# Flamingo cross-attention and experts on one core: another order of a batch, a second bank pair for the first query stack, and ranks in two matmuls

## The reference

```
x = x + tanh(g_xattn) * attention(layernorm(x), ctx, ctx)
x = x + tanh(g_ffn)   * experts(layernorm(x))

attention: q, k, v = projections with biases; softmax(q k' / sqrt(16)) v; output projection with bias
experts:   bids = sigmoid(x conf_w' + conf_b) * wealth
           the two highest bids choose two experts; weights = softmax of these two bids
           sum over the chosen experts of weight * down(silu(gate x) * up x)
```

## Time and profile before

| what | value |
|---|---|
| median of three runs | 1084.73 us (1083.6 to 1086.69) |
| the profiled execution | 1083.07 us, of which 1081.4 us is the span from first to last instruction |
| busy share of the span | PE 93%, DVE 56%, ACT 46%, POOL 34% |
| attention loop, batches 2 to 13 | 98.27 to 398.00 us of the span |
| mean granted clock of PE, share of full speed | 0.969; 1.00 in the loop |

### The profile page before, as it was taken

How to read it: one execution, slowest core, us unless ns; L and a number is a source line. 1 busy time by engine, 2 the same in 40 slices (tenths; PEclk the granted TensorE clock), 3 DMA queues, 4 the chain that set the end, 5 groups by cost and what they waited for, 6 DMA issues and landing times.

```text
span 1081.4 us, 25127 instructions
## 1 busy us (share of the span) xinstructions
PE 1001.3 (93%) x8750; PEld 855.2 (79%) x8750; DVE 610.8 (56%) x1519; ACT 502.0 (46%) x796; POOL 366.3 (34%) x439
## 2 busy tenths in 40 slices
PE   5789999999999997759999999999999999999993
PEld 4556777777777765448999999999799999999993
DVE  3556777777777776455544444444554444444452
ACT  4366777777777774334323232332433323233321
POOL 1124555555555552443322212121332212122121
PEclk8799999999999999869999999999999999999997
DMA  8000111111111119258712111121262212121211
GB/s 254 27 22 22 43 45 47 41 41 41 43 51 58 41 39 371 77 182 323 256 25 40 25 35 35 25 37 23 42 229 49 37 23 40 20 40 23 37 35 17
DMA packets 48338, 77.30 MB, mean 71 GB/s; under 512 B 8616, under 2 KB 42152, under 8 KB 44456
## 3 DMA queue, kind: packets, MB, share of 16 engines
q0 software_dynamic: 18080, 50.15, 16.7%
q1 hardware_dynamic: 30216, 26.62, 8.3%
HBM read 52.09 MB, written 24.40 MB: 71 GB/s over the span
## 4 chain that ended last, share of the span: by engine, by line
PE 81%; ACT 5%; issue 4%; DVE 3%; POOL 3%; DMA 1%; SPq 1%; POOLq 1%; ACTq 0%; DVEq 0%
PE gate L1485 17%; PE up L1485 17%; PE down L1499 11%; PE down L1501 6%; PE pv L590 4%; PE scores L579 4%; PE misc L486 4%; PE scores L540 3%; PE maxps L554 2%; PE misc L513 2%; PE misc L522 2%; POOL K_rest L1204 2%; ACT probs L771 1%; PE misc L624 1%; PE turned L1468 1%
## 5 line engine op out<-in xcount | busy, mean ns | idle before, releaser
L1937 POOL DMA_INDIRECT out<-y,token x64 | 100.9, 1577 | 424.8 <-DVE y L1806 323.8
L1696 ACT ACTIVATE silu<-gate 128x512 f32<-128x512 f32 x128 | 76.8, 600 | 281.6 <-PE up L1485 281.6
L984 DVE TENSOR_REDUCE max_neg<-maxps 128x4 f32<-128x1024 f32 x128 | 156.5, 1222 | 60.2 <-PE maxps L554 60.2
L1485 PE MATMUL gate<-x_hi,w_split 128*128 128x256 f32 x1024 | 185.0, 282 | 2.0 <-DVE x_lo L1772 1.6
L1797 DVE TENSOR_TENSOR h<-silu,up 128x512 f32<-128x512 f32 x128 | 88.1, 688 | 174.8 <-ACT silu L1696 174.8
L1499 PE MATMUL down<-w_split,h_hi 128*128 128x512 f32 x512 | 185.9, 398 | 0.0
L1485 PE MATMUL up<-x_hi,w_split 128*128 128x256 f32 x1024 | 184.4, 282 | 0.0
L771 ACT ACTIVATE probs<-scores 128x1024 f32<-128x1024 f32 x124 | 127.2, 1026 | 80.5 <-PE scores L579 79.5
L1485 PEld LDWEIGHTS gate<-x_hi,w_split 128*128 128x128 f32 x1024 | 149.4, 189 | 5.5 <-issue 2.7
L1485 PEld LDWEIGHTS up<-x_hi,w_split 128*128 128x128 f32 x1024 | 148.8, 189 | 0.0
L1501 PE MATMUL down<-w_split,h_lo 128*128 128x256 f32 x512 | 144.1, 281 | 0.0
(11 more groups left out here) (204 smaller groups left out, 1586.3 us busy)
## 6 DMA issues: line engine op xcount, KB each, us to landing
stage<-gate_up_T POOLq DMA_DIRECT2D x20, 1024.0 KB, 8.1
stage<-down_T POOLq DMA_DIRECT2D x10, 1024.0 KB, 11.1
xg<-dispatched SPq DMA_DIRECT2D x34, 272.0 KB
ctxT<-ctxT SPq DMA_DIRECT2D x17, 256.0 KB, 2.8
x_all<-x SPq DMA_DIRECT2D x16, 256.0 KB, 5.2
out<-x_all SPq DMA_DIRECT2D x16, 256.0 KB, 2.2
dispatched<-pads SPq DMA_DIRECT2D x4, 272.0 KB, 3.6
dispatched<-pads POOLq DMA_DIRECT2D x4, 272.0 KB, 4.3
```

The source lines that it names most:

```text
L984: V.tensor_reduce(to, maxps[:], AX.X, ALU.max, negate=True).then_inc(s["max_taken"], 1)
L1485: last = mm(bank[:, i, :], into_inner(w, pair, mat)[:, c, cols], r[:, c, :], start=m == 0, stop=m == len(terms) - 1)
L1696: nc.scalar.activation(silu[pair % 2][:], gate[pair % 2][:], ACT.Silu).then_inc(s_silu, 1)
L1937: pool.indirect_dma_start(out, bass.IndirectOffsetOnAxis(token[:, t:t + 1], axis=0), y[:, t, :], None, compute_op=ALU.add).then_inc(s_adde ...
```

## The change

Five things change. On TensorE the second half of a turn has another order: W1 now stands ahead of K0, Q's projection ahead of S5, each S5 to S7 ahead of its M5 to M7, W2 ahead of S7, and `logits` ahead of K1. The stack Q0 is written to the bank pair `maxps` (the new view `beside`), and so waits for no unit to be read; Q1 then waits for the read of K1, one unit less. The ranks of both halves of a batch are two matmuls with 16 columns, for which VectorE makes a second slice of `macc`: counts before the batch, and these plus the first half's. ScalarE follows the new order, and VectorE's `positions` now stand ahead of maximum 5. The new view, `stack` and `ranks`:

```
+        beside = maxps[:].rearrange("p u t s -> p (u t) s")
-            def stack(b, what, c, n):
+            def stack(b, what, c, n, to=None):
-                write_unit(n)
+                if to is None:
+                    to = scores
+                    write_unit(n)
-                for t in range(QT):
-                    mm(use.bank("RK")[:, t, 0:EXPERTS], before[:], m12[:, t, :], start=True, stop=False)
-                    if t == 1:
-                        mm(use.bank("RK")[:, t, 0:EXPERTS], ones[:], m12[:, 0, :], start=False, stop=False)
-                    last = mm(use.bank("RK")[:, t, 0:EXPERTS], ones[:], macc[:], start=False, stop=True)
-                last.then_inc(s["misc_written"], 1)
+                mm(use.bank("RK")[:, :, 0:EXPERTS], before[:], m12[:], start=True, stop=False)
+                mm(use.bank("RK")[:, :, 0:EXPERTS], ones[:], macc[:], start=False, stop=True).then_inc(s["misc_written"], 1)
```

In TensorE's `body`:

```
-                    if ahead:
-                        stack(b + 2, what[0], int(what[1]), unit(b, what))
+                    if ahead and what == BESIDE:
+                        stack(b + 2, what[0], int(what[1]), None, beside)
+                    elif ahead:
+                        stack(b + 2, what[0], int(what[1]), unit(b, what) - (1 if UNITS[UNITS.index(what) - 1] == BESIDE else 0))
...
+                weigh(b, par, 1)
                 stack_ahead("K0")
-                weigh(b, par, 1)
-                max_of_next(5)
-                score(b, par, 5)
                 if ahead:
                     project_q(use)
-                score(b, par, 6)
+                score(b, par, 5)
+                max_of_next(5)
                 if back:
                     turn_x2(b - 1, 1 - par, use)
+                score(b, par, 6)
                 max_of_next(6)
+                weigh(b, par, 2)
                 score(b, par, 7)
-                weigh(b, par, 2)
                 max_of_next(7)
-                stack_ahead("K1")
                 if back:
                     logits(use)
+                stack_ahead("K1")
                 if nxt:
                     turn_maxima(b + 1, use)
```

In ScalarE's `body`:

```
+                read_pv(b, 1)
                 stack_ahead("K0")
-                exps(b, 5)
                 if back:
                     norm_x2(b - 1, 1 - par)
-                read_pv(b, 1)
-                exps(b, 6)
+                exps(b, 5)
                 if ahead:
                     read_q(b + 2, use)
-                exps(b, 7)
+                exps(b, 6)
                 if back:
                     read_whole(x2T[:], "TX2", use)
+                exps(b, 7)
                 read_pv(b, 2)
-                stack_ahead("K1")
                 if back:
                     sigmoid(use)
+                stack_ahead("K1")
                 stack_ahead("Q0")
```

On VectorE, the end of `second_choice`, a part of `positions`, and `body`:

```
-                V.tensor_tensor(m12[:], m1[:], m2[:], ALU.add).then_inc(s["masks_ready"], 1)
+                V.tensor_tensor(m12[:], m1[:], m2[:], ALU.add).then_inc(s["masks_made"], 1)
+                dve.wait_ge(s["masks_made"], b + 1)
+                if not is_first(b):
+                    dve.wait_ge(s["rows_ready"], b)
+                V.tensor_tensor(macc[:, 1, :], macc[:, 0, :].bitcast(fp32), m12[:, 0, :].bitcast(fp32), ALU.add).then_inc(s["masks_ready"], 1)
...
-                link(V.tensor_tensor(macc[:], macc[:].bitcast(fp32), m12[:, 0, :].bitcast(fp32), ALU.add))
+                link(V.tensor_tensor(macc[:, 0, :], macc[:, 1, :].bitcast(fp32), m12[:, 1, :].bitcast(fp32), ALU.add))
                 link(V.tensor_tensor(w2[:], w1[:], ed[:], ALU.mult))
-                link(V.tensor_tensor(macc[:], macc[:].bitcast(fp32), m12[:, 1, :].bitcast(fp32), ALU.add))
...
                 max_of_next(4)
-                max_of_next(5)
                 if late:
                     positions(b - 2, par, use)
+                max_of_next(5)
```

More of the change, by code:

```diff
@@ L213, in attention_stage @@
         m12 = sb("m12", [P, QT, EXPERTS], f32r)
-        macc = sb("macc", [P, EXPERTS], f32r)
+        macc = sb("macc", [P, QT, EXPERTS], f32r)
         v1 = sb("v1", [P, QT])
@@ L287, in attention_stage @@
         STACKS = ["K0", "Q0", "K1", "Q1"]
+        BESIDE = "Q0"
         def units_before(b):
@@ L539, in stack @@
                             r = slice(half * STACK, (half + 1) * STACK)
-                            last = mm(scores[:, half * QT + i, :], picks[f"{what} {part}"][r, i, :], source[what][r, c, :],
+                            last = mm(to[:, half * QT + i, :], picks[f"{what} {part}"][r, i, :], source[what][r, c, :],
                                       start=part == "high", stop=part == "rest")
@@ L641, in known_counts @@
                 use.free(pe, "KNOWN")
-                mm(use.bank("KNOWN")[:, 0, 0:EXPERTS], ones[:], macc[:], start=True, stop=True).then_inc(s["misc_written"], 1)
+                mm(use.bank("KNOWN")[:, 0, 0:EXPERTS], ones[:], macc[:, 0, :], start=True, stop=True).then_inc(s["misc_written"], 1)
             pe.wait_ge(s["first_loaded"], 16 * NFIRST)
@@ L752, in count_rows @@
                 EPILOGUE2.free(pe, "COUNT")
-                mm(EPILOGUE2.bank("COUNT")[:, 0, 0:EXPERTS], ones[:], macc[:], start=True, stop=True).then_inc(s["misc_written"], 1)
+                mm(EPILOGUE2.bank("COUNT")[:, 0, 0:EXPERTS], ones[:], macc[:, 0, :], start=True, stop=True).then_inc(s["misc_written"], 1)
             pe.wait_ge(s["w_split"], 2)
@@ L772, in exps, with read_stack @@
                                      ACT.Exp).then_inc(s["unit_read"], 1)
-            def read_stack(par, what, c, n):
+            def read_stack(par, what, c, n, of=None):
                 to, bias = (q, 0.0) if what == "Q" else (k, ones_row[:, 0:1])
                 act.wait_ge(s["unit_written"], n + 1)
-                nc.scalar.activation(to[par][:, c * BLOCKS:(c + 1) * BLOCKS, :], scores[:], ACT.Identity,
+                nc.scalar.activation(to[par][:, c * BLOCKS:(c + 1) * BLOCKS, :], scores[:] if of is None else of, ACT.Identity,
                                      bias=bias).then_inc(s["unit_read"], 1)
@@ L869, in stack_ahead @@
                     if ahead:
-                        read_stack(par, what[0], int(what[1]), unit(b, what))
+                        read_stack(par, what[0], int(what[1]), unit(b, what), beside if what == BESIDE else None)
                 exps(b, 0)
@@ L1032, in positions @@
                 dve.wait_ge(s["second_ready"], b + 1)
-                link = chain(dve, "rows_chain", 14, b, behind=1)
+                link = chain(dve, "rows_chain", 13, b, behind=1)
                 link(V.tensor_tensor(t8[:], m1[:], u8[:], ALU.mult))
@@ L1058, in space_experts @@
                 dve.wait_ge(s["extra_known"], 1)
-                V.scalar_tensor_tensor(macc[0:1, 0:EXPERTS], extra[:], 0.0, macc[0:1, 0:EXPERTS].bitcast(fp32),
+                V.scalar_tensor_tensor(macc[0:1, 0, :], extra[:], 0.0, macc[0:1, 0, :].bitcast(fp32),
                                        ALU.max, ALU.add).then_inc(use.freed("KNOWN"), 1)
```

4 lines of the change are left out of this document (2 added, 2 removed).

## The result

The changed kernel takes 1090.56 us (median of 20 runs; one of them, 1253.93 us at a granted clock of 0.739, is a slow run and not in the ratio), against 1084.99 us for the kernel before (20 runs beside it): a ratio of 1.0049, 95% interval 1.0036 to 1.0062, so 3.9 to 6.7 us slower. The forecast was 1082.2, and its range ended at 1086.3. The profiled execution took 1091.04 us, its span 1089.4; before, 1083.07 and 1081.4. The span grew by 8.0 us, in two places. V of batch 14, which follows on the loop, starts at 400.88 where it started at 398.00: 2.9 us in the loop. From there to the last count matmul it is 71.45 us where it was 66.64: 4.8 us in the last two batches, between these two executions. The experts' stage behind it is as long as before within 0.3 us.

The account below looks back on a forecast made before the run. PE sets the pace, with DVE's ring 0.15 us behind. Eleven rings -1.65, the ring into batch 14 -0.4, batch 14 -0.3, routing -0.2: together -2.6, profiled 1080.5, median 1082.2 us; range 1078.0 to 1086.3.

Parts of the forecast that it names:

- the main fact of the forecast: In the loop, DVE is 0.15 us from being the bound: its ring takes 6.43, PE 6.58 from MT to M1.
- PE alone would need 6.15: Turned maxima (MT) to the next second maxima matmuls (M1): without DVE's bound, PE would gain some 0.43 us.
- restarts: On PE, a group of matmuls that waited runs 0.10 us longer, read from S7 and Q1.
- The routing behind the last logits: Routing after the last batch: ranks -0.34, one chained DVE step +0.2, positions -0.1; -0.2 us in all.
- the term of M1 to MT: PE's loop, M1 to MT: 1.38 us goes, 1.30 to 1.60 comes, 1.38 taken, so 18.30 stays.
- rival B: In the loop M6, M7, K1 and W1 each pay 0.10; M1 to MT grows 0.32; 1085.7 us, chance 0.15.
- 0.08 of waiting for M6, M7 and K1: Loop, M1 to MT: each comes within 0.06 us of its release; their estimated waiting in all.
- 0 to 0.30: Loop, M1 to MT: us that M6, M7 and K1 together may pay in restarts, a bound from S7's row.
- K0's saving: Loop, M1 to MT: K0's wait and restart, 0.59 us, go because K0 now stands behind a weighing.
- the 0.45 that was taken: Loop, M1 to MT: S6 waits 0.35 us for the exponential of S5 and pays a restart.
- the term of batch 15: Batch 15, where weighing 2 trades places with S7: 0 (±0.5) us.
- that of batch 14: Batch 14: S5 ahead of the maxima, ACT's exponential behind x2's normalising, which waits for GpSimd: -0.3 us (0 to -0.8).

Follow-up runs that it names:

- the short maxima: Changed kernel with batches 14 and 15 in the old order, maxima 5 and 6 taken over a quarter of each row: 1082.28 us, ratio 0.9980.
- the run with ACT's swap: Changed kernel with ACT's exponential 5 ahead of the normalising of x2 in batches 14 and 15: 1088.58 us, ratio 1.0043.
- the run with the context split moved: Kernel before with Q0 in the maxima's banks, GpSimd splitting the context ahead of the split of Q: 1082.34 us, ratio 0.9986.
- the run with K's read ahead: Kernel before with Q0 in the maxima's banks, context split ahead of Q's, two ranks, ACT's read of K ahead of exponential 3: 1080.51 us, ratio 0.9951.
- the last run: The run with K's read ahead, plus positions, maximum 4, context split and ACT's read of weighing 1 moved: 1076.37 us, ratio 0.9918.

## Why the prediction was wrong

**Right.** The ranks cost two steps of 0.11, W1 starts 0.14 behind ACT's read and waits 0.79 (0.77 forecast), and S5 to S6 is 1.62, with the wait of 0.36 that was named. No wait is left at K0, S7, Q0 or Q1. M1 waits for maximum 0, as the main fact of the forecast had it, though by 0.16 to 0.18 and not 0.3 to 0.5: "PE alone would need 6.15" counted two restarts as gained that weren't (Q1 holds PE as long as before), and PE alone needs 6.33 (S1 at 253.33, and 0.34). The piece MT to M1 is 6.51 in both bodies, where the mean of 6.50 and 6.35 was taken: so the gain is 0.07 a ring and not 0.15, because from the copy of the maxima to the last step of the statistics it takes 3.9 in both bodies now (272.99 to 276.90 in the second, 3.74 before). The routing behind the last logits is 0.23 shorter (464.07 to 472.33, before 456.15 to 464.64), where 0.2 was taken.

**The step that failed in the loop** is the term of M1 to MT, "and so no change in this piece". It measured +0.33, rival B's +0.32, and the period of 25.14 lies above the 24.9 at which B was to be read. Its mechanism was only half B's. The text took 0.08 of waiting for M6, M7 and K1, and "0 to 0.30" for restarts, of which it took 0.08 (1.38 less 1.30). In fact M6 and M7 wait 0.10 and 0.05 for DVE, and W2 and the logits behind them pay 0.10 to 0.12 each, which the short maxima gave back. What the forecast didn't follow is why they come so close to DVE. From M5 over its maximum to M6 it takes 1.72 (241.70 to 243.42), and from M6 to M7 1.83. Before, M5 stood 3.66 ahead of M6 (238.33 to 241.99). Now M5 stands behind S5 and M6 behind S6; S5 to S6 takes 1.62, so DVE's 1.72 is the longer, by 0.10.

**The restart was too broad a rule.** It was read from S7, K0 and Q1. But K0 and Q1 still hold PE for 0.67 in the changed kernel, without a wait ahead of them (238.76 to 239.43, 249.32 to 249.99), and so does K1, which took 0.56 behind M7 and takes 0.66 behind the logits. That is what a stack costs behind a weighing or the logits, so 0.10 of K0's saving was never to be had, and K1 lost 0.10 by its new place. The logits ahead of it lost 0.07 (0.99 from 245.69 to 246.68, before 0.92). Against these, S6 cost 0.09 less than the 0.45 that was taken. And in the run with short maxima S6 waited 0.29 by its bracket, 0.36 by the steps, with no restart behind it, while in the changed kernel 0.10 was paid behind M6 and M7, which waited 0.10 and less. The Trainium skill, in "TensorE: Matmul & The Clock Gate", section "Step-by-step: what each phase is for", has weight loads pulled ahead of matmuls in flight. By that rule the first is to be expected and the second isn't. Which waits pay stays open.

**The step that failed in the tail** is the term of batch 15, "0 (±0.5)"; that of batch 14, "-0.3", left out the clock. Both go by PE's places without the clock and without what stands behind a waiting instruction. Batch 14 (M1 to MT) took 18.43 instead of 17.34, but 1.52 of that is four groups that ran wholly or in part at the clock's lower level (0.17 for the transposes ahead of W0, W0 1.87 instead of 1.00, and 0.25 and 0.23 for S3 and M3 behind it). Without it the batch would be 16.91, an estimate by this subtraction, so 0.43 gained, within the "0 to -0.8"; the run with ACT's swap, whose W0 took 1.07, has 16.79. But the clock isn't the new order's alone: seven of the nine profiles with PE's old order have 18.86 to 20.36 there, with W0 or a group behind it at the lower level. In batch 15 the stretch from S0 to W3 took 21.66 (426.56 to 448.22) instead of 18.50 (423.11 to 441.61), because S6 and all that follows it stand behind the transposes of x2, which wait 1.94. The text had weighed ACT's late exponential 5, but not that PE holds S6 back by itself. How much of the tail's loss the clock alone took stays open: no run changes the clock and nothing else.

**The median.** The 8.0 us between the two profiled spans are more than the 5.6 us between the medians, since the profiled run of before was a quick one. The forecast corrected its total for that, but with the loop's 2.9 us taken off, 2.7 us of the 5.6 are left for the last two batches, not 4.8.

## What to carry to other kernels

A gap between two groups that share banks through another engine is a ring of its own: before a reorder, write down for each pair (maximum to maximum, score to score) how long the reader needs, and check it against the new distance, not only against the waits that are there today. An instruction moved behind one that waits inherits the wait together with all that follows it, so in the last iterations, where the cover is gone, the order wants its own look. And where one ring is a tenth of a microsecond from being last, look for the next one before counting the gain: here, ring after ring, the period went from 24.88 over 24.86, 24.77 and 24.70 to 24.35 us, and only all the edits together gave 0.8%.

## What the hardware showed that was not expected

A wait needn't show as idle time: M6 and M7 of the changed kernel start 0.05 behind the end of the maximum that they need, yet carry no bracket. The step from one group to the next, held against the same step elsewhere, found them.

The granted clock of the tail differs between kernels with the same waits. In the run with the context split moved, PE waits in batch 14 as before (0.69 at S2, 0.69 at W1, then 0.29 at M5, 1.11 at S6 and 0.47 at the transposes of x2; before 0.69, 0.69, 0.28, 1.12 and 0.47), yet the granted clock falls to 0.50 from those transposes on (410.98), where before it stayed at 1.00 past MT; the stretch to the count took 71.06 us, with the old order, more than the changed kernel's in the run with ACT's swap (70.47). So a tail of 66.6 us at a clock of 0.90 in one profile is not a fixed quantity.

GpSimd can hold up DVE. In the run with K's read ahead, a DVE step on 128x16 elements took 1.13 us instead of 0.17:

```profile
234.72 1.13 DVE L1043 TENSOR_TENSOR t<-m,u 128x16 f32<-128x16 f32 x1
```

while POOL split the context:

```profile
234.55 1.27 POOL L1201 TENSOR_TENSOR ctx_rest<-ctxT,ctx_high 128x512 fp32r<-128x512 f32 x1 [0.15 <-POOL ctx_high L1199]
```

It ends with POOL's instruction (235.85 against 235.82). In the run ahead of it, on GpSimd's split alone, the same step took 0.95 and ended with the split too, while the DVE step just ahead of it, with one input in PSUM, took 0.17 inside the split. In the last run, where the two no longer meet, the same step takes 0.17. The Trainium skill, "Advanced Engine Details and Errata", "GPSIMD Details", says that GpSimd shares a read and a write interface with DVE and conflicts with its instructions that have two SBUF inputs; this step has two, and the trace agrees.
